# Gated cross-attention and FFN on one core: an order list per engine, centring on ScalarE, one set of columns for the weighted sum

## What is computed

```
h      = (x - mean(x)) / sqrt(var(x) + 1e-5)                    # 4 x 256 x 256, fp32
scores = h @ ctx.T / sqrt(256);  masked keys -> -1e30           # 256 x 1601 a batch
x      = x + tanh(g_xattn) * softmax(scores) @ ctx
h2     = (x - mean(x)) / sqrt(var(x) + 1e-5)
x      = x + tanh(g_ffn) * ((gelu(h2 @ W0) * (h2 @ W1)) @ W2)    # operands rounded to fp8, hidden 1024
```

## Time and profile before

| what | value |
|---|---|
| device time, median of 3 runs | 150.0 us (149.98 to 152.47) |
| profiled execution, first to last instruction | 149.9 us |
| busy: PE / weight load / DVE / ACT / POOL | 130.0 / 106.3 / 126.9 / 71.2 / 74.8 us |
| mean granted TensorE clock | 0.966 |
| HBM read and written | 11.57 MB and 1.05 MB |

### The profile page before, as it was taken

How to read it: one execution, slowest core, us unless ns; L and a number is a source line. 1 busy time by engine, 2 the same in 40 slices (tenths; PEclk the granted TensorE clock), 3 DMA queues, 4 the chain that set the end, 5 groups by cost and what they waited for, 6 DMA issues and landing times.

```text
span 149.9 us, 2277 instructions
## 1 busy us (share of the span) xinstructions
PE 130.0 (87%) x786; PEld 106.3 (71%) x786; DVE 126.9 (85%) x255; ACT 71.2 (47%) x131; POOL 74.8 (50%) x52
## 2 busy tenths in 40 slices
PE   7389967998769799983999799939999899999992
PEld 5179847996757699873887798828889777344781
DVE  1458999999999999899699998996899696988752
ACT  3075319799225466920254559410541592557300
POOL 2106892769999905379997010599990100100000
PEclk9978999999999999999699999995999999999999
DMA  1599930059300591000301300000000000000133
GB/s 41 219 376 385 377 145 4 0 165 350 124 0 0 179 413 42 4 0 17 123 0 7 133 0 4 2 0 0 0 4 0 2 0 0 0 4 0 35 115 130
DMA packets 6754, 12.75 MB, mean 85 GB/s; under 512 B 852, under 2 KB 4696, under 8 KB 6744
## 3 DMA queue, kind: packets, MB, share of 16 engines
q1 hardware_dynamic: 6456, 12.62, 24.2%
q10 hardware_dynamic: 288, 0.00, 0.1%
HBM read 11.57 MB, written 1.05 MB: 84 GB/s over the span
## 4 chain that ended last, share of the span: by engine, by line
PE 50%; DVE 36%; DMA 5%; issue 4%; ACT 2%; SPq 1%; DVEq 0%
PE ring L580 12%; PE pv L615 11%; PE scores L654 7%; DVE act L428 6%; PE pv L619 6%; DVE wc L497 5%; DMA cn<-in_ctx_dram 5%; DVE wc L496 5%; DVE pT_lo L436 4%; PE ring L668 4%; DVE sp L446 3%; PE scores L600 3%; PE scores L601 3%; PE scores L595 3%; DVE cT_lo L436 2%
## 5 line engine op out<-in xcount | busy, mean ns | idle before, releaser
L334 POOL TENSOR_TENSOR chl<-cn,chl 128x1024 fp32r<-128x1024 f32 (+1 forms) x16 | 31.9, 2006 | 4.0 <-ACT chl L376 3.8
L369 ACT ACTIVATE pT_hi<-ring 128x512 fp32r<-128x512 f32 (+1 forms) x32 | 15.7, 514 | 36.3 <-PE ring L580 36.3
L615 PE MATMUL pv<-chl,pT_hi 128*128 128x512 f32 (+1 forms) x104 | 32.5, 427 | 0.0
L600 PE MATMUL scores<-cT_lo,xT_hi 128*128 128x512 f32 (+2 forms) x64 | 21.9, 350 | 6.6 <-DVE cT_lo L436 6.6
L601 PE MATMUL scores<-cT_hi,xT_lo 128*128 128x512 f32 (+2 forms) x64 | 21.7, 346 | 0.0
L436 DVE TENSOR_TENSOR pT_lo<-ring,pT_hi 128x512 fp32r<-128x512 f32 (+1 forms) x32 | 18.1, 582 | 3.7 <-ACT pT_hi L369 3.7
L619 PEld LDWEIGHTS pv<-chl,pT_lo 128*128 128x128 f32 (+1 forms) x104 | 16.9, 200 | 5.8 <-issue 1.9
L615 PEld LDWEIGHTS pv<-chl,pT_hi 128*128 128x128 f32 (+1 forms) x104 | 19.0, 199 | 2.7
L619 PE MATMUL pv<-chl,pT_lo 128*128 128x256 f32 (+1 forms) x104 | 18.3, 296 | 2.7 <-DVE pT_lo L436 2.7
L382 ACT ACTIVATE sp<-sp,nb 128x1024 f32<-128x1024 f32 (+1 forms) x16 | 15.4, 962 | 9.7 <-DVE nb L452 9.7
L580 PE MATMUL ring<-ident,sp 128*128 128x128 f32 (+1 forms) x104 | 16.5, 285 | 2.8 <-ACT sp L382 2.8
(11 more groups left out here) (58 smaller groups left out, 203.9 us busy)
## 6 DMA issues: line engine op xcount, KB each, us to landing
cn<-in_ctx_dram SPq DMA_DIRECT2D x12, 512.0 KB, 6.5
ws<-in_L_ffn_w_gating_dram SPq DMA_DIRECT2D x4, 512.0 KB, 7.2
ws<-in_L_ffn_w_linear_dram SPq DMA_DIRECT2D x2, 512.0 KB, 3.8
out_dram<-xs SPq DMA_DIRECT2D x8, 128.0 KB, 1.7
mrow<-in_mask_BxS_bk_dram SPq DMA_DIRECT2D x4, 200.1 KB, 6.8
xs<-in_x_dram SPq DMA_DIRECT2D x1, 768.0 KB, 9.2
cn<-in_ctx_dram SPq DMA_DIRECT2D x4, 65.0 KB
xs<-in_x_dram SPq DMA_DIRECT2D x1, 256.0 KB, 4.2
```

What stands on the lines that cost most here:

```text
L334: nc.gpsimd.tensor_tensor(chl[b % 2][0:parts, t0:t1, D:2 * D], cn[b % 2][0:parts, t0:t1, :], chl[b % 2][0:parts, t0:t1, 0:D].bitcast(f32), ...
L369: nc.scalar.activation(dst, bank_view(f, size), ACT.Copy).then_inc(hi_ready, 1)
L600: nc.tensor.matmul(dst, xT_hi[:, j, k, :], cT_lo[:, k, cols], start=False, stop=False)
L615: return nc.tensor.matmul(pv[:, :], pT_hi[0:parts, t, :], chl[b % 2][0:parts, t, :], start=(t == 0), stop=(t == NT - 1))
```

## The change

1. **Lists.** The common list becomes four: TensorE, ScalarE, VectorE and GpSimd each have a list of their own, with every unit of all four batches written out. Semaphore counts are looked up in the list of the engine that signals. T is now called P.
2. **Centring.** K moves to ScalarE, as two `Identity` activations with bias -mean; F gives `sr` = (256(var+eps))^-0.5 and its negative, which the exponential takes as its scale and the maximum as its factor. G has one more small DVE instruction, F one more small POOL instruction.
3. **Weighted sum.** The hi·lo product goes to the same 256 columns of `pv` as the other two: three matmuls of 256 columns a context tile for one of 512 and one of 256. A has one large addition less (L467), and its two `tensor_tensor` instructions of 128x1 become `tensor_scalar`.
4. N's copy to fp8 moves from DVE to ScalarE. The tanh of the gates is computed after the first exponential, its loads go through SyncE behind batch 1's, and a context group is loaded as soon as that group is used up. Batch 0's first group comes in two halves, with the mask behind it. `pT_hi` and `pT_lo` have two buffers; TensorE does 20 warming matmuls for 18.

```diff
-    START = """ ... """   MIDDLE = """ ... """   END = """ ... """
+    PE_ORDER = """
+        C0:0 C0:1 X0 C0:2 C0:3 S0:0 C0:6 S1:0 C0:5 C0:4 S0:1 C1:1 S1:1 X1 C1:0 S0:2 C1:3 S0:3 S1:2 C1:2 S1:3
+        C1:4 S2:0 C1:5 S3:0 P0:0 P0:1 S2:1 C1:6 V0:0 P0:3 P0:2 S3:1 S2:2 P1:1 P1:3 S2:3 P1:0 V0:1 V0:2 C2:3
+        V0:3 P1:2 S3:2 C2:1 S3:3 V1:0 C2:5 C2:6 V1:1 X2 C2:0 V1:2 C2:2 V1:3 P2:0 S4:0 P2:1 P3:3 S5:0 S4:1
+        C2:4 V2:0 P3:0 P2:2 S5:1 V2:1 P2:3 P3:1 S4:2 S4:3 X3 P3:2 V2:2 V2:3 C3:0 S5:2 C3:2 C3:3 S5:3 V3:0
+        C3:5 C3:1 C3:4 V3:1 V3:2 C3:6 V3:3 S6:0 P4:0 S6:1 S6:2 N0 P4:1 S6:3 P4:3 P4:2 V4:0 P5:0 P5:1 S7:0
+        S7:1 V4:1 V4:2 P6:2 V4:3 S7:2 P6:3 S7:3 P5:3 P5:2 V5:0 V5:1 P6:0 N1 V5:2 V5:3 P6:1 H0 H1 P7:0 P7:1
+        V6:0 V6:1 V6:2 V6:3 P7:3 P7:2 H2 V7:0 V7:1 V7:2 V7:3 H3 N2 H4 H5 H6 N3 H7 H8 H9 H10 H11 Y0 H12 H13
+        H14 Y1 H15 Y2 Y3 Y4 Y5 Y6 Y7"""
+    DVE_ORDER = """
+        G0 C0:0 C0:1 X0 C0:2 C0:3 G1 G2 C0:6 C0:4 C0:5 M0:0 C1:1 M1:0 X1 C1:0 M0:1 C1:3 M1:1 C1:2 C1:4 W0
+        C1:5 P0:0 P0:1 M2:0 G3 P0:3 C1:6 P0:2 W1 P1:3 M3:0 P1:1 M2:1 P1:0 A0 C2:3 P1:2 U0 C2:1 C2:5 M3:1
+        C2:6 X2 C2:0 C2:2 A1 P3:3 P2:0 P2:1 W2 W3 M4:0 C2:4 P3:0 U1 P2:2 M5:0 P2:3 P3:1 M4:1 X3 P3:2 A2 C3:0
...
+    ACT_ORDER = """
+        K0 C0:0 C0:1 X0 R0:1 C0:2 C0:3 R0:3 R0:2 R0:0 C0:6 C0:4 C0:5 K1 C1:1 C1:0 X1 C1:3 C1:2 R1:3 C1:4
+        E0:0 C1:5 E1:0 P0:0 P0:1 E0:1 C1:6 E1:1 P0:3 P0:2 R1:0 P1:3 R1:1 P1:0 P1:1 R1:2 C2:3 E2:0 P1:2 K2
...
+    POOL_ORDER = """
+        F0 B0 Z0:1 Z0:3 F1 F2 B1 Z0:0 Z0:2 I0 I1 Z1:1 Z1:3 Z1:2 Z1:0 B2 Z2:3 I2 Z2:0 Q0 I3 B3 F3 Z2:1 Z2:2
+        Z3:1 Q1 I4 Z3:0 Z3:2 Z3:3 Q2 I5 Q3"""
...
+            def centre(b):
+                actor.wait_ge(mean_ready, n_mean[("G", b)])
+                for j in range(QT * b, QT * (b + 1)):
+                    last = nc.scalar.activation(xc[:, j, :], xs[:, j, :], ACT.Identity, bias=negm[:, j:j + 1], scale=1.0)
+                last.then_inc(centred, 1)
...
                 nc.scalar.activation(sp[:, j % 2, cols], sp[:, j % 2, cols], ACT.Exp, bias=nb[:, j:j + 1],
-                                     scale=SCALE, accum_out=rs[:, j, h:h + 1]).then_inc(exp_ready, 1)
+                                     scale=sr[:, j:j + 1], accum_out=rs[:, j, h:h + 1]).then_inc(exp_ready, 1)
...
-            def normed(j):
-                nc.vector.tensor_scalar(xn[:, j, :], xs[:, j, :], mv[:, j, 0:1], rstd[:, j:j + 1],
-                                        ALU.subtract, ALU.mult).then_inc(xn_ready, 1)
+                nc.vector.tensor_scalar(negm[:, j:z], mv[:, j:z, 0], -1.0, None, ALU.mult)
+                nc.vector.tensor_scalar(ve[:, j:z], mv[:, j:z, 1], EPS, float(D), ALU.add, ALU.mult).then_inc(mean_ready, 1)
...
-                link(nc.vector.tensor_tensor(rt[:, j:j + 1], rs[:, j, 0:1], rs[:, j, 1:2], ALU.add))
+                link(nc.vector.tensor_scalar(rt[:, j:j + 1], rs[:, j, 0:1], rs[:, j, 1:2], None, ALU.add))
                 link(nc.vector.reciprocal(ri[:, j:j + 1], rt[:, j:j + 1]))
-                link(nc.vector.tensor_tensor(fo[:, j:j + 1], ri[:, j:j + 1], vt[:, j:j + 1], ALU.mult))
+                link(nc.vector.tensor_scalar(fo[:, j:j + 1], ri[:, j:j + 1], seen[:, j:j + 1], tg[:, 0:1],
+                                             ALU.mult, ALU.mult))
                 dve.wait_ge(pv_done, j + 1)
-                link(nc.vector.scalar_tensor_tensor(out=xs[:, j, :], in0=pv[:, D:2 * D], scalar=fo[:, j:j + 1],
-                                                    in1=xs[:, j, :], op0=ALU.mult, op1=ALU.add))
                 nc.vector.scalar_tensor_tensor(out=xs[:, j, :], in0=pv[:, 0:D], scalar=fo[:, j:j + 1],
                                                in1=xs[:, j, :], op0=ALU.mult, op1=ALU.add).then_inc(pv_used, 1)
...
+                pe.wait_ge(c_hi, n_chi[("R", b, g)])
+                pe.wait_ge(hi_ready, n_hi[f])
+                for t in range(t0, t1):
+                    nc.tensor.matmul(pv[:, 0:D], hi[0:parts, t, :], chl[b % 2][0:parts, t, 0:D],
+                                     start=(t == 0), stop=False)
+                pe.wait_ge(c_lo, n_clo[("Z", b, g)])
+                for t in range(t0, t1):
+                    nc.tensor.matmul(pv[:, 0:D], hi[0:parts, t, :], chl[b % 2][0:parts, t, D:2 * D],
                                      start=False, stop=False)
+                pe.wait_ge(lo_ready, n_lo[f])
+                for t in range(t0, t1):
+                    last = nc.tensor.matmul(pv[:, 0:D], lo[0:parts, t, :], chl[b % 2][0:parts, t, 0:D],
+                                            start=False, stop=(t == NT - 1))
```

More of the change, by code:

```diff
@@ L86, in gated_cross_attention_ffn @@
[L86 to L97, removed]
@@ new lines, in gated_cross_attention_ffn @@
+    fills = [s for s in pe_order if s[0] in "XCPN"]
+    at = {f: i for i, f in enumerate(fills)}
+    n_filled = count(pe_order, "XCPN")
+    n_scored = {(s[1], s[2] // 2): i + 1 for i, s in enumerate(s for s in pe_order if s[0] == "S" and s[2] % 2 == 1)}
+    unit = {(s[1], s[2] // 2): i for i, s in enumerate(s for s in pe_order if s[0] == "S" and s[2] % 2 == 0)}
+    unit_of = {u: s for s, u in unit.items()}
+    n_centred = count(act_order, "K")
+    n_hi = count(act_order, "XCP")
+    n_chi = count(act_order, "R")
@@ new lines, in gated_cross_attention_ffn @@
+    n_exp = count(act_order, "E")
+    n_x2 = count(act_order, "N")
+    n_mean = count(dve_order, "G")
+    n_lo = count(dve_order, "XCP")
+    n_masked = count(dve_order, "M")
+    n_nb = {s[1]: i + 1 for i, s in enumerate(s for s in dve_order if s[0] == "M" and s[2] == 1)}
+    n_var2 = count(dve_order, "U")
+    n_xn2 = count(dve_order, "L")
+    n_wc = count(dve_order, "W")
+    n_scale = count(pool_order, "F")
+    n_bias = count(pool_order, "B")
+    n_clo = count(pool_order, "Z")
+    n_rstd2 = count(pool_order, "Q")
@@ L105, in gated_cross_attention_ffn @@
+    n_w = count(pool_order, "I")
     with ExitStack() as stack:
@@ L163, in gated_cross_attention_ffn @@
         pv = ps("pv", [P, BANK], f32)
-        spare = [(at[("N", B - 1)] + i) % RING for i in range(RING)]
+        spare = [(len(fills) - 1 + i) % RING for i in range(RING)]
         hbanks = [(scores[:, 0, :], scores[:, 1, :]), (scores[:, 2, :], scores[:, 3, :]), (ring[spare[1]][:, :], pv[:, :])]
@@ L213, in group, with group_fills, landed @@
             return (GT * g, min(GT * g + GT, NF), P) if g < NG - 1 else (NF, NT, TAIL)
+        def group_fills(b, g):
+            return [("C", b, KD * g + k) for k in range(KD)] if g < NG - 1 else [("C", b, CF - 1)]
+        def landed(b, g):
+            return 16 * (b // 2 + 1 + (1 if b % 2 == 0 and g == 0 else 0))
         def split_out(f, hi):
@@ L350, in _ @@
             nc.gpsimd.tensor_copy(ident16[:], ident[:]).then_inc(ident_ready, 1)
-            for s in order:
+            for s in pool_order:
                 if s[0] == "F":
-                    first_rstd(s[1])
+                    score_scale(s[1])
                 elif s[0] == "B":
@@ L395, in gelu @@
                                      ACT.Gelu_apprx_tanh).then_inc(gate_ready, 1)
-            for s in order:
-                if s[0] in "XCT":
+            gated = False
+            for s in act_order:
+                if s[0] == "K":
+                    centre(s[1])
+                elif s[0] in "XCP":
                     fill_hi(s)
@@ L661, in project @@
                 half, q = divmod(j, HALF // P)
+                if j == 0:
+                    pe.wait_ge(w_ready, max(n_w[("I", c)] for c in range(WC)))
                 if j < 2:
-                    pe.wait_ge(freed, len(fills))
+                    bank_free(fills[-1 if j == 0 else -2])
                 else:
                     pe.wait_ge(y_added, j - 1)
-                pe.wait_ge(act_ready, HT * (half + 1))
                 for t in range(HT):
+                    if t >= HT - 2:
+                        pe.wait_ge(act_ready, HT * half + t + 1)
                     last = nc.tensor.matmul(ybank[j % 2][:, 0:D], act[:, half, t, P * q:P * (q + 1)], w2[:, t, :],
```

306 lines of the change are left out of this document (148 added, 158 removed).

## The result

The changed kernel takes 135.83 us (median of 4 runs, 134.3 to 136.98) against 150.21 us before (4 runs): 0.897 of the time, 95% interval 0.887 to 0.908. A second set on another chip gave 135.29 us and 0.896 (0.889 to 0.904). The forecast was 137.5 us, with 133.5 to 141 around it and a range of 133 to 146, so the time lies inside both. In some executions, whatever the kernel, the core takes over 1.5% longer than in the quickest; the ratios leave those out, the medians do not.

The account below looks back on a forecast made before the run. VectorE, slowed by waits for GpSimd, was taken as the bound, TensorE afterwards. A floor of 130.0 us plus losses of 3 at the start and 4.5 in middle and end gave 137.5 us, forecast 133.5 to 141, range 133 to 146.

Parts of the forecast that it names:

- The bound and its change: Middle batches: VectorE, with waits for GpSimd, bounds; after the change it has 22.6 us of work against TensorE's 24.4.
- the W pair: Two VectorE instructions for the low parts: taken to stay at 2.19 + 2.23 us when GpSimd is in the way.
- The weighted sum: TensorE: a context tile goes from 0.233 + 0.12 to 0.36 us, weight loads hidden, +0.8 us in all.
- The start: Up to the M3:0 row maximum, put at 38 us: TensorE's loss 3 us, for 9.3 before.
- The gates' loads: Moved behind batch 1's loads, with the wait for them behind the first exponential only: costed at nothing.
- The sum: TensorE's 119.5 us of work within a floor of 130.0, plus losses of 3 and 4.5: 137.5 us.
- The middle: Middle and end: a TensorE loss of 1.5 us a batch for the old 6, 4.5 over three batches.
- cover for W2 and W3: Two back-to-back VectorE low-part units, up to 8.9 us, taken as covered by 8.4 us of queued TensorE work.
- The second: VectorE's new one-column instructions wait for GpSimd too, 7.7 us come back: 142 us, chance 0.08.
- The fourth rival: Added weight loads of the weighted-sum products are not hidden, 20.9 us on TensorE: 158 us, chance 0.06.
- The first: Fixed lists starve an engine, two thirds of the old loss stay, 3 us a batch: 144 us, chance 0.20.
- The third: No gain: GpSimd's list becomes the bound or loads arrive late: 147 to 153 us, chance 0.09.

Follow-up runs that it names:

- experiment 3: Changed kernel with only the two one-column VectorE instructions given two tensor inputs in SBUF again: 145.10 us, 0.961 of the kernel before.
- experiment 4: Changed kernel with only the centring moved back from ScalarE to VectorE: 145.67 us, lowest 143.91.
- experiment 5: Changed kernel with the old common list, 512-column product, second addition and N's copy on VectorE; centring on ScalarE and one-tensor-input one-column instructions stay: 146.40 us, 0.972 of before.
- experiment 7: Changed kernel with the hi x lo products of the weighted sum issued twice, 104 more matmuls of 256 columns: 144.77 us.
- experiment 9: Changed kernel with the gates' two loads issued first from ScalarE's queue again: 136.47 us, against the changed kernel's 135.29 in the same set.
- experiment 1: Changed kernel with the one common order list of the kernel before for all four engines, changed operations kept: 139.49 us, 0.923 of before.
- experiment 10: Changed kernel with batch 1's second normalisation moved three items up VectorE's list: 133.39 us; with batch 0's mask also loaded behind context group 1: 132.82 us.
- experiment 2: Changed kernel's four lists with the old operations (centring, N's copy, 512-column product, two additions, two-input one-column instructions): 155.22 us, 1.027 of before.
- experiment 8: Changed kernel with only the first loads undone, batch 0's first context group in one DMA and mask behind all its context: 136.75 us.

## Why the prediction was right, step by step

**The bound and its change: right.** VectorE had been the bound, by waits for GpSimd and by plain work; with most of both gone TensorE is. Experiments 3 and 4 each put one kind of wait back and lose 8 to 9 us, and experiment 5 shows that the plain work counted as well. What was not priced is the clock: the waits of 4 to 5 us are followed by products at half pace (experiments 3 and 4), so that such a wait avoided is worth more than its length. VectorE's busy time was put at 102.9 us and is 101.0, which is partly luck: the W pair, costed as unchanged, takes 7.0 us less, and L, costed as unchanged, 3.9 more. The centring on ScalarE was put at 0.41 to 0.6 us and takes 0.50; the exponential's scale at 0 to 0.2 and takes 0.09 (1238 ns, for 1152 in the kernel before). The Trainium skill (ScalarE: Activation LUTs, "What ACT_TABLE_LOAD costs") gives about 93 ns for each operand that is a column; the trace agrees, with 86 ns.

**The weighted sum: right.** All three groups of the changed kernel run at 0.47 to 0.48 us for four, from its chain of waits (start, us, engine, tile, line); experiment 7 prices another 104 products at 0.09 us each, weight load included.

```profile
...
84.87 0.47 PE pv L633 x4
85.34 0.47 PE pv L637 x4
85.81 0.48 PE pv L641 x4
...
```

**The start: the cause missed, the size half right.** M3:0 was put at 38 us and came at 35.12. (The prediction calls M3 the third row-maximum pair; it is the fourth, and both times are M3's.) The gates' loads were costed at nothing, and moving them behind the others lets x land 1.45 us earlier (experiment 9). The sum kept the old 7.92 us for the first transposes. They came at 5.48 in this execution, at up to 7.31 in others with the same loads. Most of such a gain goes at once into the next wait, for context group 1, with which I had not reckoned:

```profile
...
5.48 1.06 PE L601 MATMUL ring<-ident,cn 128*128 128x128 f32 x8 [0.40 <-DMA cn<-in_ctx_dram]
...
9.36 1.06 PE L601 MATMUL ring<-ident,cn 128*128 128x128 f32 x8 [2.38 <-DMA cn<-in_ctx_dram]
...
```

**The middle: the term that was mis-sized.** I took a loss of 1.5 us a batch; between 34 and 83 us it is nothing. My reason, that two engines with 2 us between them don't run without gaps, did not hold, and not only thanks to the lists: under the common list TensorE is idle for 2.0 us in the 76 us from 35 to 111 (experiment 1), against the 4.5 taken for three batches. VectorE's 2 us less of work a batch was enough. What I had counted as cover for W2 and W3 (8.4 us) held: VectorE gave 4.0 us to them from 51.75, and TensorE did not stop.

```profile
...
51.75 0.68 DVE L521 TENSOR_SCALAR wc<-ws 128x1024 uint16<-128x1024 uint16 x1
52.47 0.43 DVE L522 TENSOR_SCALAR wc<-wc 128x1024 bf16<-128x1024 bf16 x1
52.81 0.69 DVE L521 TENSOR_SCALAR wc<-ws 128x1024 uint16<-128x1024 uint16 x1
53.53 2.26 DVE L522 TENSOR_SCALAR wc<-wc 128x1024 bf16<-128x1024 bf16 x1
...
```

**The sum.** It was made for a span as if for a time. For the span it gave 137.5, and 132.4 was measured. The terms of the 5.1 us are: 2.4 for the first transposes (7.92 taken, 5.48 found), 0.6 for the loss at the start (3 taken, 2.4 found, the wait for group 1), 2.6 for the middle and end (4.5 taken, 1.9 found, at L1), less 0.3 for a longer tail. They make 5.3; the 0.2 left over are small gaps and the rounding of the prices. As a span, 132.4 us would lie below the whole range. That the time came so close to the forecast is luck in two ways: time exceeds span by 1.9 us, and the middle run takes 1.5 us more than the profiled one.

**A step left out.** L was costed as unchanged, since it had never waited before (0.44 us at most). Its two instructions of batch 1, 4.60 us together, are the one wait for GpSimd that holds TensorE in the changed kernel, and experiment 10 takes it back. The earlier trace rows would have told me to look up every VectorE form in the new place of its list, not only those that had waited in the old one.

**The rivals.** The second (one-column instructions wait) did not happen, but its price, 4.5 us above the forecast, was half of what experiment 3 measured: I had priced the mean wait and not the one in front of `pv`. The Trainium skill (SBUF — State Buffer, "Who interferes with whom") lets `tensor_scalar` contend with GpSimd when its operands meet the conditions of a two-port mode. For one column nothing of it is seen: 16 of them stayed at 0.20 to 0.28 us, and no one-column `tensor_scalar` of the other kernels took longer. For 128x256 to fp8 the trace agrees: L1 waited 2.20 and 2.48 us, with 0.41 of work. The fourth rival (unhidden loads) is ruled out. The first did not come in the changed kernel; experiment 2 shows what it would look like, lists and operations that don't fit. The third did not come: no wait of TensorE is put down to GpSimd.

## What to carry to other kernels

Busy time of VectorE beside a busy GpSimd may be waiting; compare the shortest and the mean duration of one form, and look at what GpSimd runs at that moment. Price such a wait by what is queued behind the instruction, not by its mean: one factor of a column, waiting in front of the only accumulation bank, cost 5 us of TensorE, and 2.9 more at half the clock behind it. An order list and the operations that it orders are one change: neither can be judged, or moved to another kernel, alone. And loads that nobody waits for belong behind those that somebody does: two tiny ones held x back, though what that cost here is not shown.

## What the runs showed of the hardware

- A VectorE instruction with two tensor inputs in SBUF can wait for several GpSimd instructions, not only for the one in flight: `fo` 5.07 us on one column, over the last three of four that came without a gap (experiment 3); the first of an fp32 `tensor_scalar` pair 3.74 us, over two (experiment 4). `rt`, 1.8 us before that `fo`, and the 2.00 us of the earlier trace rows ended with one instruction. What decides between the two was not tried.
- `tensor_scalar` on 128x1 never took more than 0.28 us in any kernel here. On 128x2, normally 0.17, it took 1.76 us in experiment 5 and 1.89 in experiment 8, beside GpSimd.
- After TensorE had stood idle for 4 to 5 us, its granted clock was 0.50, 1.2 of 2.4 GHz, for the next 4 to 6 us, and four products of 256 columns took 1.0 us for 0.47 (experiments 3 and 4).
- A 128x256 `tensor_scalar` with fp8 output waits as well (up to 2.48 us an instruction), which the kernel before had not shown (0.44 us at most).
- Two loads of 0.5 KB, issued first from another queue, delay the landing of a 256 KB load by 1.45 us (experiment 9).
- Device time is the span plus 1.8 to 1.9 us in all runs of this single-core kernel that list both.
